# Local attention: scores for 32 queries against their 160 keys, q and k through one scratch tensor, and another order on VectorE

## The chip, the cores and the metric

The kernel runs on one core of a Trainium2 chip. The metric is the time of one execution on the device in microseconds (us). All data are float32.

## What is computed

The reference adds two blocks to x (2 sequences of 4096 tokens, 256 channels): a recurrent attention with 16 heads, and a two-layer local transformer. Only the second one is touched. Cut to it:

```
for l in range(2):                       # DEPTH
    h = shift_token(x);  q, k, v = split(h @ wqkv[l])        # 8 heads of 64
    q, k = rotary_xpos(l2norm(q) * qs, l2norm(k) * ksc)
    # windows of 128 tokens; a query sees its own window and the one before
    sim = einsum('bhwid,bhwjd->bhwij', bq * 8, bk)           # 128 x 256
    mask = (i < j) | (i > j + 128) | (j == -1)
    attn = softmax(where(mask, -max, sim));  o = attn @ bv
    x = x + o @ wo[l]
    h = layernorm(shift_token(x)) * lg + lb
    a, g = split(h @ w1[l] + b1);  x = x + (a * gelu(g)) @ w2[l] + b2
```

A query at place i sees the keys i-128 to i. So 32 neighbouring queries together see 160 keys, and 127 of the 256 places in each row of the square are masked.

## The kernel before

The program runs setup, mix, scan, gate and then local, one stage after another. The local stage (`local_stage`) works through T / 128 = 32 windows for each of two layers (NW = 32, u counts 64 of them), for two streams s = 0, 1 (the two sequences). One call of `half(s, u, w, l)` on each engine is the work on attention of stream s in window u together with the second part (values, wo, layer norm, MLP) of the other stream `o = 1 - s` in the window `um`, and the projections for the next window. There are 128 halves. `w` is the parity of the window, `un = um + 1` the other stream's next window. Each engine has its own written order of steps; semaphores tie them together.

In a half, for stream s: TensorE computes the scores of four pairs of heads (`scores`, `hp` = 0 to 3); VectorE adds the mask and takes the row maximum (`row_max`); ScalarE takes the exponent with the row sum (`exponent`); VectorE inverts the sum (`inverse_sums`), GpSimd scales P by it (`normalise`), and VectorE turns P in blocks of 32 x 32 (`turn_p`). The blocks still have to change places between groups of partitions, which goes through DRAM: SP writes two pairs at a time to scratch `pz` (`write_p`, g = 0, 1) and reads each back with four DMAs, one for 32 partitions (`read_p`). In the next half TensorE multiplies the result, `pT`, with V (`values`): pairs 0 and 1 into bank D ahead of the other stream's first scores, pairs 2 and 3 into bank B between its scores of pair 1 and pair 2.

q and k go the same way: `turn_q`, `write_q`, `read_q` and `turn_k`, `write_k`, `read_k`, through scratch `qz` and `kz`. All of these DMAs are issued by SP, in this order within a half:

```
read_q(o, un) | store, load_rot, load_window | write_p(s, u, 0)
write_k(o, un) | write_p(s, u, 1) | read_p(s, u, 0) | read_k(o, un, wn)
read_p(s, u, 1) | write_q(s, u + 1)
```

SP works in order: a DMA behind a wait is not issued before the wait is over. TensorE's order in a half is values 0 and 1 (of o), scores 0 and 1 (of s), values 2 and 3, scores 2 and 3, wo, then the projections with the mean and the variance between them (`mean` is L2529, `variance` L2533), and the MLP (L2551, L2559). `deviate` on VectorE waits for the mean.

## Time and profile before

| | |
|---|---|
| median of 3 runs | 4971.94 us (4968.18 to 4976.64) |
| the profiled execution | 4966.22 us, span 4964.4 us, mean granted TensorE clock 0.959 |
| local stage | from about 2257 us to the end |
| busy, whole span | TensorE 4507.8 us, its weight loads 3817.4, VectorE 3564.7, ScalarE 2979.7, GpSimd 2441.6 |
| DMA queue of SP | 53.1% of the 16 engines' span |

PE is TensorE, PEld its weight loads, DVE VectorE, ACT ScalarE, POOL GpSimd, SPq the DMAs that SP issues. A wait stands in brackets behind the instruction that ended it. Issuing a DMA does not count as busy time.

### The profile page before, as it was taken

The numbers are of one execution on the slowest core, as the hardware profiler recorded it, in microseconds if no ns is written. First come the engines' busy times: TensorE is split into PE (matmuls) and PEld (weight loads), VectorE is DVE, ScalarE is ACT, GpSimd is POOL, SyncE is SP. The second block draws the span as 40 slices with busy tenths as digits, with TensorE's granted clock in tenths as the row PEclk, the third lists the DMA queues.
The fourth block names the chain that finished last, engine by engine and source line by source line (L and its number), as shares of the span: only waits on it lengthen the run. The fifth ranks groups of instructions, "written<-read, shape, count | busy, mean of one in ns | idle before, by whom it ended". The sixth has DMA issues, their size and how long they took to land. (4 is left out here: it accounts for less than half of the span.)

```text
span 4964.4 us, 269505 instructions
## 1 busy us (share of the span) xinstructions
PE 4507.8 (91%) x107928; PEld 3817.4 (77%) x107928; DVE 3564.7 (72%) x10345; ACT 2979.7 (60%) x8486; POOL 2441.6 (49%) x3196
## 2 busy tenths in 40 slices
PE   7898898678888888666999999999999999999998
PEld 6888888678888888654777777777777777777777
DVE  4666666568878887475777777777777777777775
ACT  5777777534444444354666666666666666666665
POOL 1222222267777777203555555555555555555554
PEclk8999999789999999788999999999999999999999
DMA  2343343467777777694555666555565555555554
GB/s 87 87 96 93 93 98 89 114 143 165 165 165 163 167 164 161 175 299 126 170 170 168 173 174 171 172 171 171 180 196 175 173 173 172 171 171 173 173 175 131
DMA packets 1283528, 775.96 MB, mean 156 GB/s; under 512 B 686800, under 2 KB 1179088, under 8 KB 1282256
## 3 DMA queue, kind: packets, MB, share of 16 engines
q1 hardware_dynamic: 1231888, 700.43, 53.1%
q10 hardware_dynamic: 51392, 73.02, 5.0%
q14 instruction: 190, 1.56, 0.1%
q8 instruction: 58, 0.95, 0.1%
HBM read 410.44 MB, written 362.68 MB: 156 GB/s over the span
## 5 line engine op out<-in xcount | busy, mean ns | idle before, releaser
L2367 ACT ACTIVATE l_prob<-l_prob,l_nb,l_rq 128x256 f32<-128x256 f32 x1024 | 601.6, 590 | 20.8 <-DVE l_nb L2193 13.1
L2033 POOL TENSOR_TENSOR l_prob<-l_prob,l_rinv 128x512 f32<-128x512 f32 x512 | 526.8, 1039 | 108.4 <-DVE l_rinv L2173 108.4
L2017 POOL TENSOR_TENSOR l_k<-l_kn,l_tab 128x512 f32<-128x512 f32 x128 | 162.5, 1270 | 614.8 <-DVE l_kn L2165 614.8
L2559 PE MATMUL lD<-l_hid,w 128*128 128x128 f32 x3072 | 364.0, 275 | 0.0
L2559 PEld LDWEIGHTS lD<-l_hid,w 128*128 128x128 f32 x3072 | 353.3, 192 | 0.0
L2551 PEld LDWEIGHTS lA<-l_hn,w 128*128 128x128 f32 x2048 | 242.9, 195 | 110.1 <-POOL l_hn L2051 61.1
L2202 DVE STREAM_TRANSPOSE l_pb<-l_prob 128x512 f32<-128x512 f32 x512 | 326.6, 676 | 0.6 <-POOL l_prob L2033 0.5
L2027 POOL TENSOR_TENSOR l_qr<-l_q 128x512 f32<-128x512 f32 x128 | 162.4, 1269 | 328.1 <-DVE l_q L2131 328.1
L1097 POOL TENSOR_TENSOR sc_aqx<-sc_late,sc_headmask 128x256 f32<-128x256 f32 x256 | 170.8, 667 | 278.9 <-PE sc_Y L1190 277.2
L1173 PE MATMUL sc_AB<-sc_aq,sc_bkx 32*32 32x32 f32 x16384 | 257.3, 198 | 37.4 <-POOL sc_bkx L1097 29.1
L497 POOL TENSOR_TENSOR rk<-rk,bkraw 128x256 f32<-128x256 f32 x64 | 54.6, 871 | 477.9 <-DVE bkraw L383 477.9
L2551 PE MATMUL lA<-l_hn,w 128*128 128x128 f32 x2048 | 266.0, 284 | 11.8 <-POOL l_hn L2051 5.2
L1115 POOL TENSOR_TENSOR sc_bkT<-sc_tok,sc_headmask 128x128 f32<-128x128 f32 x512 | 263.2, 534 | 0.0
L2524 PE MATMUL lD<-l_oT,wo 128*128 128x128 f32 x2048 | 262.6, 281 | 0.1
L2524 PEld LDWEIGHTS lD<-l_oT,wo 128*128 128x128 f32 x2048 | 238.2, 191 | 29.2 <-issue 28.9
L2473 PE MATMUL lB<-wqkv,l_h 128*128 128x512 f32 x512 | 242.9, 597 | 17.4 <-DVE l_mask L2262 17.2
L2551 PE MATMUL lB<-l_hn,w 128*128 128x128 f32 x2048 | 250.9, 276 | 0.0
L1173 PEld LDWEIGHTS sc_AB<-sc_aq,sc_bkx 32*32 32x32 f32 x16384 | 213.3, 108 | 39.4 <-issue 38.6
L2473 PE MATMUL lC<-wqkv,l_h 128*128 128x512 f32 x512 | 241.0, 593 | 0.0
L2473 PE MATMUL lA<-wqkv,l_h 128*128 128x512 f32 x512 | 240.9, 593 | 0.0
L2551 PEld LDWEIGHTS lB<-l_hn,w 128*128 128x128 f32 x2048 | 240.5, 193 | 0.0
L2193 DVE TENSOR_TENSOR l_nb<-l_mx,l_nrq 128x2 f32<-128x2 f32 x512 | 220.6, 431 | 17.7
(276 smaller groups left out, 13707.3 us busy)
## 6 DMA issues: line engine op xcount, KB each, us to landing
scratch_pz<-l_pb SPq DMA_DIRECT2D x256, 512.0 KB, 3.0
l_pT<-scratch_pz SPq DMA_DIRECT2D x1024, 128.0 KB, 3.2
scratch_cm<-cm SPq DMA_DIRECT2D x64, 512.0 KB, 4.1
scratch_qz<-l_q SPq DMA_DIRECT2D x128, 256.0 KB, 2.9
l_qT<-scratch_qz SPq DMA_DIRECT2D x512, 64.0 KB, 2.0
scratch_kz<-l_k SPq DMA_DIRECT2D x128, 256.0 KB, 2.8
l_kT<-scratch_kz SPq DMA_DIRECT2D x512, 64.0 KB, 2.9
sc_early<-scratch_cm ACTq DMA_DIRECT2D x59, 512.0 KB, 4.7
```

The lines of the kernel that those rows point to most:

```text
L1097: return nc.gpsimd.tensor_tensor(dst[:], src.unsqueeze(2).broadcast_to([P, 2 * BG, HQ, CH]), headmask[:].unsqueeze(1).unsqueeze(3).broadca ...
L1115: last = nc.gpsimd.tensor_tensor(bkT[c % 2][:, b * BG:(b + 1) * BG], tok[k][:, c, b, 1:3].rearrange("p x g i -> p (x g) i").unsqueeze(2) . ...
L1173: last = mm(AB_ps[c][at, (x * BG + q) * QH:(x * BG + q + 1) * QH], bkx[c][at, 2 * q + x].rearrange("p h t -> p (h t)"), aq[c][at, q], star ...
L2017: tt(k1[s][:], kn[s][:], wide(2, slice(0, DH)), ALU.mult)
L2033: tt(prob[s][:, pair], prob[s][:, pair], rinv[s][:, pair].unsqueeze(2).broadcast_to([P, 2, 2 * P]), ALU.mult).then_inc(Q["pn"][s].sem, 1)
L2193: tt(nb[s][:, pair], mx[s][:, pair], nrq8[s][:, pair], ALU.mult).then_inc(Q["nb"][s].sem, 1)
L2202: nc.vector.transpose(pb[s][:, g, :, at:at + 2].rearrange("p j h x t -> p (h x) j t"), prob[s][:, 2 * hp:2 * hp + 2].rearrange("p h (x j k ...
L2367: last_ = nc.scalar.activation(prob[s][:, h], prob[s][:, h], ACT.Exp, scale=rq8[s][:, h:h + 1], bias=nb[s][:, h:h + 1], accum_out=sums[s][ ...
L2473: last_ = mm(bank[s][j][:], h[:, k * P:(k + 1) * P], wqkv[:, k, j * INNER:(j + 1) * INNER], start=(k == 0), stop=(k == CC - 1))
L2524: last_ = mm(bank[s][3][:, m * P:(m + 1) * P], wo[:, k, m * P:(m + 1) * P], oT[s][:, k], start=(k == 0), stop=(k == NHP - 1))
L2551: last_ = mm(bank[s][j][0:MW, at:at + P], w1[:, k, tile * MW:(tile + 1) * MW], hn[s][:, k], start=(k == 0), stop=(k == CC - 1))
L2559: last_ = mm(bank[s][3][:, c * P:(c + 1) * P], w2[:, m, c * P:(c + 1) * P], hid[s][:, m], start=(c == 0 and m == 0), stop=(c == CC - 1 and ...
```

## The change

- **Scores.** One matmul of 64 x 128 by 256 columns for each head becomes four of 64 x 32 by 160, one for each block i of 32 queries, into 32 partitions of the same bank. `prob`, the exponent, the scaling and the turn have 160 columns for each head instead of 256.
- **Mask.** `winmask` holds both cases, and `mask`, its preparation and `remask` are gone.
- **q and k.** Both are turned into one tile `qk`, written by one DMA to `qkz` and read by four. `qkT` holds three windows' places: the keys of a window with w = 0 are read twice, into places 2 (with q) and 0, so that the 160 keys always lie side by side.
- **P.** `pz` holds 5 blocks of 32 keys for each 32 queries. `read_p` has to place them by absolute key block in `pT`: two DMAs for each group of 32 partitions, of j + 1 and 4 - j runs.
- **VectorE's order.** `turn_k` goes ahead of `inverse_sums` 2, `turn_p` 0 ahead of `deviate`, `turn_p` 1 ahead of `inverse_sums` 3.

```diff
+    NR = BL + 1
+    SPAN = 32 * NR
...
-        qT, kT = two("qT", [P, P, NHP]), two("kT", [P, 2, BL, NHP, 32])
-        V, prob = two("V", [P, 2, HEADS, DH]), two("prob", [P, HEADS, 2 * P])
-        pb, pT = two("pb", [P, 2, BL, NHP, 2, 32]), two("pT", [P, 2, BL, NHP, 2, 32])
+        qk, qkT = two("qk", [P, BL, 2, NHP, 32]), two("qkT", [P, 3 * BL, 2, NHP, 32])
+        V, prob = two("V", [P, 2, HEADS, DH]), two("prob", [P, HEADS, SPAN])
+        pb, pT = two("pb", [P, 2, NR, NHP, 32]), two("pT", [P, 2, BL, 2, NHP, 32])
...
-                def write_q(s, u):
+                def write_qk(s, u):
 
                     sp.wait_ge(S["q_turned"][s].sem, S["q_turned"][s].after(u))
                     sp.sem_inc(sems["free"], 1)
-                    sp.wait_ge(S["qT"][s].sem, S["qT"][s].after(u, 1))
+                    sp.wait_ge(S["k_turned"][s].sem, S["k_turned"][s].after(u))
                     sp.sem_inc(sems["free"], 1)
-                    sp.dma_start(a["qz"][s], q1[s][:].rearrange("p h d -> p (h d)")).then_inc(S["q_out"][s].sem, 16)
-
-                def read_q(s, u):
-                    sp.wait_ge(S["q_out"][s].sem, S["q_out"][s].after(u))
+                    sp.wait_ge(S["qkT"][s].sem, S["qkT"][s].after(u, 1))
+                    sp.sem_inc(sems["free"], 1)
+                    if not isinstance(u, int) or u > 1:
+                        sp.wait_ge(S["kT"][s].sem, S["kT"][s].after(u - 1))
+                        sp.sem_inc(sems["free"], 1)
+                    sp.dma_start(a["qkz"][s], qk[s][:].rearrange("p j y h t -> p (j y h t)")).then_inc(S["qk_out"][s].sem, 16)
+
+                def read_qk(s, u, w):
+
+                    sp.wait_ge(S["qk_out"][s].sem, S["qk_out"][s].after(u))
                     sp.sem_inc(sems["free"], 1)
                     sp.wait_ge(Q["sc"][s].sem, Q["sc"][s].after(u * NHP - 1))
                     sp.sem_inc(sems["free"], 1)
+                    turned = a["qkz"][s].rearrange("(i c) (j n) -> j c i n", i=BL, j=BL)
+                    cur = (2, 1)[w] * BL
                     for j in range(BL):
-                        sp.dma_start(qT[s][32 * j:32 * j + 32].rearrange("p (i t) h -> p i (t h)", i=BL),
-                                     a["qz"][s].rearrange("(i c) (j n) -> j c i n", i=BL, j=BL)[j]).then_inc(S["qT"][s].sem, 16)
-
-                def write_k(s, u):
-                    sp.wait_ge(S["k_turned"][s].sem, S["k_turned"][s].after(u))
-                    sp.sem_inc(sems["free"], 1)
-                    sp.wait_ge(S["kT"][s].sem, S["kT"][s].after(u, 1))
-                    sp.sem_inc(sems["free"], 1)
-                    sp.dma_start(a["kz"][s], k1[s][:].rearrange("p h d -> p (h d)")).then_inc(S["k_out"][s].sem, 16)
-
-                def read_k(s, u, w):
-                    sp.wait_ge(S["k_out"][s].sem, S["k_out"][s].after(u))
-                    sp.sem_inc(sems["free"], 1)
-                    sp.wait_ge(Q["sc"][s].sem, Q["sc"][s].after(u * NHP - 1))
-                    sp.sem_inc(sems["free"], 1)
-                    for j in range(BL):
-                        sp.dma_start(kT[s][32 * j:32 * j + 32, w].rearrange("p i h t -> p i (h t)"),
-                                     a["kz"][s].rearrange("(i c) (j n) -> j c i n", i=BL, j=BL)[j]).then_inc(S["kT"][s].sem, 16)
+                        sp.dma_start(qkT[s][32 * j:32 * j + 32, cur:cur + BL].rearrange("p i y h t -> p i (y h t)"),
+                                     turned[j]).then_inc(S["qkT"][s].sem, 16)
+                    if w == 0:
+                        for j in range(BL):
+                            sp.dma_start(qkT[s][32 * j:32 * j + 32, 0:BL, 1].rearrange("p i h t -> p i (h t)"),
+                                         turned[j][:, :, 32 * NHP:]).then_inc(S["kT"][s].sem, 16)
...
+                    n, row = 32 * NHP, 32 * NHP * NR
+                    at = (s * 2 + g) * P * row
                     for j in range(BL):
-                        sp.dma_start(pT[s][32 * j:32 * j + 32, g].rearrange("p i h x t -> p i (h x t)"),
-                                     a["pz"][s, g].rearrange("(i c) (j n) -> j c i n", i=BL, j=BL)[j]).then_inc(H[g]["pT"][s].sem, 16)
+                        for slot, lo, hi in ((0, 0, j + 1), (1, j, BL)):
+                            start = at + lo * 32 * row + (j + BL * slot - lo) * n
+                            sp.dma_start(pT[s][32 * j:32 * j + 32, g, lo:hi, slot].rearrange("p i h t -> p i (h t)"),
+                                         bass.AP(a["pz"].tensor, start, [[row, 32], [32 * row - n, hi - lo], [1, n]])
+                                         ).then_inc(H[g]["pT"][s].sem, 16)
...
-                    if within(un):
-                        read_q(o, un)
...
                     write_p(s, u, 0)
                     if within(un):
-                        write_k(o, un)
+                        write_qk(o, un)
                     write_p(s, u, 1)
                     read_p(s, u, 0)
                     if within(un):
-                        read_k(o, un, wn)
+                        read_qk(o, un, wn)
                     read_p(s, u, 1)
...
-                    if within(u + 1):
-                        write_q(s, u + 1)
...
-                        for t in (kT[s], V[s]):
+                        for t in (qkT[s], V[s], pT[s]):
                             nc.gpsimd.memset(t[:], 0.0)
                         nc.gpsimd.memset(hid[s][:, FULL, :], 0.0)
                         nc.gpsimd.memset(x1[s][1][:], 0.0)
-                        nc.gpsimd.memset(mask[s][0][:], MASKED)
...
+                    dve.wait_ge(S["qk_out"][s].sem, S["qk_out"][s].after(u, 1))
+                    nc.vector.transpose(qk[s][:, :, 0].rearrange("p j h t -> p h j t"),
...
-                                                               in1=mask[s][w][:].rearrange("p x n -> p (x n)"), scale=1.0, scalar=3 * MASKED,
+                                                               in1=wm[:, int(u in (0, NW))], scale=1.0, scalar=3 * MASKED,
...
-                    nc.vector.transpose(pb[s][:, g, :, at:at + 2].rearrange("p j h x t -> p (h x) j t"),
-                                        prob[s][:, 2 * hp:2 * hp + 2].rearrange("p h (x j k) -> p (h x) j k", x=2, j=BL)
+                    nc.vector.transpose(pb[s][:, g, :, at:at + 2].rearrange("p r h t -> p h r t"),
+                                        prob[s][:, 2 * hp:2 * hp + 2].rearrange("p h (r k) -> p h r k", r=NR)
...
-                def remask(s, u, w):
-                    if w == 0:
-                        at = u if isinstance(u, int) else None
-                        dve.wait_ge(Q["mx"][s].sem, Q["mx"][s].after(u * NHP + NHP - 1))
-                        if at == NW - 2:
-                            nc.vector.memset(mask[s][0][:, 1, :], MASKED).then_inc(S["mask0"][s].sem, 2)
-                        else:
-                            nc.vector.tensor_copy(mask[s][0][:, 1, :], wm[:, 0:P]).then_inc(S["mask0"][s].sem, 2)
...
                     inverse_sums(s, u, 1)
+                    if within(un):
+                        turn_k(o, un)
                     inverse_sums(s, u, 2)
+                    turn_p(s, u, 0)
                     if mlp:
                         deviate(o, um, wm_)
+                    turn_p(s, u, 1)
                     inverse_sums(s, u, 3)
-                    turn_p(s, u, 0)
-                    turn_p(s, u, 1)
-                    if within(un):
-                        turn_k(o, un)
                     turn_p(s, u, 2)
                     turn_p(s, u, 3)
...
-                    for x in range(2):
-                        rows_ = slice(x * DH, (x + 1) * DH)
-                        last_ = mm(scored(s, hp, x), qT[s][rows_, :, hp], kT[s][rows_, :, :, hp].rearrange("p x i t -> p (x i) t"),
-                                   start=True, stop=True)
+                        pe.sem_inc(sems["free_pe"], 1)
+                    own, back = (2, 1)[w] * BL, (1, 0)[w] * BL
+                    for i in range(BL):
+                        for x in range(2):
+                            rows_ = slice(x * DH, (x + 1) * DH)
+                            last_ = mm(scored(s, hp, x)[32 * i:32 * i + 32], qkT[s][rows_, own + i, 0, hp],
+                                       qkT[s][rows_, back + i:back + i + NR, 1, hp], start=True, stop=True)
                     last_.then_inc(Q["sc"][s].sem, 1)
...
-                            last_ = mm(valued(s, hp)[x * DH:(x + 1) * DH], V[s][:, slot, 2 * hp + x], pT[s][:, g, :, at + x, slot],
+                            last_ = mm(valued(s, hp)[x * DH:(x + 1) * DH], V[s][:, (1 - w, w)[slot], 2 * hp + x], pT[s][:, g, :, slot, at + x],
...
-    q, kx = np.arange(P)[:, None], np.arange(P)[None, :]
-    neg = np.float32(MASKED)
-    before, own = np.where(kx < q, neg, 0), np.where(kx > q, neg, 0)
-    out["winmask"] = np.concatenate([before, own], axis=1).astype(np.float32)
+    row, r = np.arange(P)[:, None], np.arange(160)[None, :]
+    neg, behind = np.float32(MASKED), r - row % 32
+    near = np.where((behind < 0) | (behind > P), neg, 0)
+    begin = np.where(r < P - row // 32 * 32, neg, near)
+    out["winmask"] = np.stack([near, begin], axis=1).astype(np.float32)
```

SP's DMAs of one half in the local stage, before. The names are out<-in; behind them stands the shape, in which 32x4x256 is 32 partitions by 4 runs of 256 elements:

```order
L1924 DMA scratch_pz<-l_pb 128x1024
L1907 DMA scratch_kz<-l_k 128x512
L1924 DMA scratch_pz<-l_pb 128x1024
L1932 DMA l_pT<-scratch_pz 32x4x256 x4
L1915 DMA l_kT<-scratch_kz 32x4x128 x4
L1932 DMA l_pT<-scratch_pz 32x4x256 x4
L1891 DMA scratch_qz<-l_q 128x512
```

The same place with the change, in a half with wn = 0 (in the others L1912 is missing), up to the start of the second read of P, which has the same seven rows as the first:

```order
L1921 DMA scratch_pz<-l_pb 128x640
L1897 DMA scratch_qkz<-l_qk 128x1024
L1921 DMA scratch_pz<-l_pb 128x640
L1933 DMA l_pT<-scratch_pz 32x128
L1933 DMA l_pT<-scratch_pz 32x4x128
L1933 DMA l_pT<-scratch_pz 32x2x128
L1933 DMA l_pT<-scratch_pz 32x3x128 x2
L1933 DMA l_pT<-scratch_pz 32x2x128
L1933 DMA l_pT<-scratch_pz 32x4x128
L1933 DMA l_pT<-scratch_pz 32x128
L1908 DMA l_qkT<-scratch_qkz 32x4x256 x4
L1912 DMA l_qkT<-scratch_qkz 32x4x128 x4
```

Between the writes of P and the second read of P stood 8 reads; now 12 or 16 stand there, and the second read is 8 itself.

VectorE between the residual sum of the other stream (`attended`) and the end of the turns of P, before:

```order
L2219 TENSOR_TENSOR l_x_0<-lD,l_h_0 128x2x128
L2173 RECIPROCAL l_rinv<-l_sums 128x2 x2
L2228 TENSOR_TENSOR l_dev<-l_x_0,lD 128x256
L2173 RECIPROCAL l_rinv<-l_sums 128x2
L2202 STREAM_TRANSPOSE l_pb<-l_prob 128x4x4x32 x2
L2158 STREAM_TRANSPOSE l_k<-l_kr 128x4x4x32
L2202 STREAM_TRANSPOSE l_pb<-l_prob 128x4x4x32 x2
```

The same with the change:

```order
L2202 TENSOR_TENSOR l_x_0<-lD,l_h_0 128x2x128
L2167 RECIPROCAL l_rinv<-l_sums 128x2
L2152 STREAM_TRANSPOSE l_qk<-l_kr 128x4x4x32
L2167 RECIPROCAL l_rinv<-l_sums 128x2
L2194 STREAM_TRANSPOSE l_pb<-l_prob 128x2x5x32
L2211 TENSOR_TENSOR l_dev<-l_x_0,lD 128x256
L2194 STREAM_TRANSPOSE l_pb<-l_prob 128x2x5x32
L2167 RECIPROCAL l_rinv<-l_sums 128x2
L2194 STREAM_TRANSPOSE l_pb<-l_prob 128x2x5x32 x2
```

The turn of k and of pair 0 now stand ahead of the deviation (`l_dev`), that of pair 1 right behind it.

## Rows read from the trace of the kernel before

**Rows 1.** The head of the page
```profile
span 4964.4 us, 269505 instructions
```

**Rows 2.** Windows, 3000 to 3600 us: busy us PE, PEld, DVE, ACT, POOL; clock
```profile
3000.00:3600.00 600.00, 593.89 (x4349) 464.02 (x4350) 441.36 (x1503) 396.95 (x1083) 325.98 (x366) 1.00 0.59 173
```

**Rows 3.** PE timeline, one half and the next: start us, us, what, [idle before <-releaser]
```profile
3515.77 1.09 PE L2516 MATMUL lD<-l_pT,l_V 128*64 128x128 f32 x16
3516.80 0.60 PE L2498 MATMUL lB<-l_kT,l_qT 64*128 64x256 f32 x1
...
3517.47 0.63 PE L2498 MATMUL lA<-l_kT,l_qT 64*128 64x256 f32 x4
3518.72 1.09 PE L2516 MATMUL lB<-l_pT,l_V 128*64 128x128 f32 x16 [0.62 <-DMA l_pT<-scratch_pz]
...
3520.99 2.05 PE L2524 MATMUL lD<-l_oT,wo 128*128 128x128 f32 x16
...
3524.60 0.38 PE L2529 MATMUL lD<-l_x1s,l_mean_w 128*128 128x128 f32 x2
...
3539.83 1.09 PE L2516 MATMUL lB<-l_pT,l_V 128*64 128x128 f32 x16 [1.06 <-DMA l_pT<-scratch_pz]
```

**Rows 4.** Timeline of DVE in the same half
```profile
3525.02 0.42 DVE L2228 TENSOR_TENSOR l_dev<-l_x,lD 128x256 f32<-128x256 f32 x1 [1.07 <-PE lD L2529]
...
3525.43 1.28 DVE L2202 STREAM_TRANSPOSE l_pb<-l_prob 128x512 f32<-128x512 f32 x2
```

**Rows 5.** Timeline of SP's queue in the same half
```profile
3526.87 0.34 SPq L1924 DMA_DIRECT2D scratch_pz<-l_pb  x1
...
3531.39 1.74 SPq L1932 DMA_DIRECT2D l_pT<-scratch_pz  x4
3533.32 1.73 SPq L1915 DMA_DIRECT2D l_kT<-scratch_kz  x4
3535.22 1.73 SPq L1932 DMA_DIRECT2D l_pT<-scratch_pz  x4
```

**Rows 6.** First and last start of the value matmuls (source view of their line)
```profile
L2516 PE MATMUL lD<-l_pT,l_V x2048: 272/273/476, 2308.1 to 4940.7; 128*64 128x128 f32 x187
```

**Rows 7.** Waits of PE, 2400 to 4900 us: total, times, longest
```profile
PE lB L2516 <- DMA l_pT<-scratch_pz: 6.8, 11, 1.3
```

**Rows 8.** One read of P on SP (source view): ns min/median/max
```profile
L1932 SPq DMA_DIRECT2D l_pT<-scratch_pz x1024: 302/432/1631, 2303.0 to 4935.4; - x171
```

**Rows 9.** DMA issues of the page: KB each, median us to landing
```profile
scratch_pz<-l_pb SPq DMA_DIRECT2D x256, 512.0 KB, 3.0
l_pT<-scratch_pz SPq DMA_DIRECT2D x1024, 128.0 KB, 3.2
...
l_qT<-scratch_qz SPq DMA_DIRECT2D x512, 64.0 KB, 2.0
```

**Rows 10.** The page's costliest groups: busy us, mean ns of one
```profile
L2367 ACT ACTIVATE l_prob<-l_prob,l_nb,l_rq 128x256 f32<-128x256 f32 x1024 | 601.6, 590 | 20.8 <-DVE l_nb L2193 13.1
L2033 POOL TENSOR_TENSOR l_prob<-l_prob,l_rinv 128x512 f32<-128x512 f32 x512 | 526.8, 1039 | 108.4 <-DVE l_rinv L2173 108.4
...
L2202 DVE STREAM_TRANSPOSE l_pb<-l_prob 128x512 f32<-128x512 f32 x512 | 326.6, 676 | 0.6 <-POOL l_prob L2033 0.5
...
L1173 PE MATMUL sc_AB<-sc_aq,sc_bkx 32*32 32x32 f32 x16384 | 257.3, 198 | 37.4 <-POOL sc_bkx L1097 29.1
```

**Rows 11.** Timeline of SP in the scan stage: four DMAs of 512 runs each
```profile
1518.32 2.35 SPq L1025 DMA_DIRECT2D sc_part<-scratch_inv  x4
```

**Rows 12.** PE timeline in the gate stage, before the local stage
```profile
2225.66 1.89 PE L1707 MATMUL ga_O<-ga_wos,ga_z 128*128 128x256 f32 x8
...
2230.44 1.11 PE L1699 MATMUL ga_Y<-ident,ga_yt 128*128 128x128 f32 x4 [2.36 <-DMA ga_yt<-scratch_y_tok]
2231.34 3.09 PE L1707 MATMUL ga_O<-ga_wos,ga_z 128*128 128x256 f32 x8
```

**Rows 13.** GpSimd's timeline at the start of the local stage
```profile
2256.95 0.95 POOL L2069 MEMSET l_kT<- 128x1024 f32 x1 [225.59 <-POOLq L104]
```

More of the change, by code:

```diff
@@ L1761, in local_stage @@
         rot, tab = two("rot", [P, 4, DH]), two("tab", [P, 4, DH])
-        wm = one("wm", [P, 2 * P])
+        wm = one("wm", [P, 2, SPAN])
         mean_w, pause, least = one("mean_w", [P, P]), one("pause", [P, NB]), one("least", [P, 1])
         x1s, dsqs = two("x1s", [P, P]), two("dsqs", [P, P])
-        mask = [two(f"mask{s}_", [P, 2, P]) for s in range(NB)]
         hT = [two(f"h{s}_", [P, CC, P + 1]) for s in range(NB)]
@@ L1780, in local_stage @@
         bank = [[ctx.enter_context(nc.psum_tensor(f"l{n}{s}", [P, 512], F32)) for n in "ABCD"] for s in range(NB)]
-        sems = {n: ctx.enter_context(nc.semaphore(f"l_{n}")) for n in ("wm", "set", "prep", "zero", "free", "wqkv", "wo", "w1", "w2", "wiped0", "wiped1")}
+        sems = {n: ctx.enter_context(nc.semaphore(f"l_{n}")) for n in ("wm", "set", "zero", "free", "free_pe", "wqkv", "wo", "w1", "w2", "wiped0", "wiped1")}
         R = signals(nc, ctx, "tab", 1, "lr")
         S = signals(nc, ctx, "q_ps k_ps v_ps qsq ksq v_sb ss_q ss_k clamped ln_n rn rq8 kn qm qr k12 kr q_turned k_turned "
-                    "q_out:16 k_out:16 qT:64 kT:64 mask0 wo_ps carry x1 x1_sum mean_ps dev dsq dsq_sum var_ps ln_v rstd hn w2_ps hout "
+                    "qk_out:16 qkT:64 kT:32 wo_ps carry x1 x1_sum mean_ps dev dsq dsq_sum var_ps ln_v rstd hn w2_ps hout "
                     "out:16", 2, "l")
@@ L1789, in local_stage @@
         O = signals(nc, ctx, "oT", 2, "lg", ahead=4)
-        H = [signals(nc, ctx, "p_out:16 pT:64", 2, f"lg{g}_") for g in range(2)]
+        H = [signals(nc, ctx, "p_out:16 pT:128", 2, f"lg{g}_") for g in range(2)]
         I = [signals(nc, ctx, "h_in:8 rot_in:8", 2, f"li{w}_") for w in range(2)]
@@ L1846, in scored @@
         def scored(s, hp, x):
-            return ((bank[s][1], bank[s][2]), (bank[s][0], bank[1 - s][0]))[hp % 2][x][:, 0:2 * P]
+            return ((bank[s][1], bank[s][2]), (bank[s][0], bank[1 - s][0]))[hp % 2][x][:, 0:SPAN]
         def valued(s, hp):
@@ L2015, in rotate_k @@
                     pool.wait_ge(S["kr"][s].sem, S["kr"][s].after(u, 1))
-                    pool.wait_ge(S["k_out"][s].sem, S["k_out"][s].after(u, 1))
                     tt(k1[s][:], kn[s][:], wide(2, slice(0, DH)), ALU.mult)
@@ L2032, in normalise @@
                     pair = slice(2 * hp, 2 * hp + 2)
-                    tt(prob[s][:, pair], prob[s][:, pair], rinv[s][:, pair].unsqueeze(2).broadcast_to([P, 2, 2 * P]), ALU.mult
+                    tt(prob[s][:, pair], prob[s][:, pair], rinv[s][:, pair].unsqueeze(2).broadcast_to([P, 2, SPAN]), ALU.mult
                        ).then_inc(Q["pn"][s].sem, 1)
@@ L2125, in rotate_q @@
                     dve.wait_ge(S["qr"][s].sem, S["qr"][s].after(u, 1))
-                    dve.wait_ge(S["q_out"][s].sem, S["q_out"][s].after(u, 1))
                     q = bank[s][0][:].rearrange("p (h d) -> p h d", h=HEADS)
@@ L2157, in turn_k @@
                     dve.wait_ge(S["kr"][s].sem, S["kr"][s].after(u))
-                    nc.vector.transpose(k1[s][:].rearrange("p h d -> p (h d)").rearrange("p (j h t) -> p h j t", j=BL, h=NHP),
+                    dve.wait_ge(S["qk_out"][s].sem, S["qk_out"][s].after(u, 1))
+                    nc.vector.transpose(qk[s][:, :, 1].rearrange("p j h t -> p h j t"),
                                         kr[s][:].rearrange("p h d -> p (h d)").rearrange("p (h j c) -> p h j c", h=NHP, j=BL)
@@ L2181, in row_max @@
                     dve.wait_ge(Q["p_turned"][s].sem, Q["p_turned"][s].after(n, NHP))
-                    if hp == 0 and w == 0:
-                        dve.wait_ge(S["mask0"][s].sem, S["mask0"][s].after(u, 1))
                     nc.vector.memset(pause[:, s:s + 1], 0.0)
@@ L2260, in first @@
                     for s in range(NB):
-                        nc.vector.tensor_copy(mask[s][0][:, 0, :], wm[:, P:2 * P])
-                        last = nc.vector.tensor_copy(mask[s][1][:].rearrange("p x n -> p (x n)"), wm[:])
-                    last.then_inc(sems["prep"], 1)
-                    dve.wait_ge(sems["prep"], 1)
-                    for s in range(NB):
                         sum_k(s, 0)
@@ L2480, in scores @@
                     if hp == 0:
-                        pe.wait_ge(S["qT"][s].sem, S["qT"][s].after(u))
-                        pe.wait_ge(S["kT"][s].sem, S["kT"][s].after(u))
+                        pe.wait_ge(S["qkT"][s].sem, S["qkT"][s].after(u))
+                        pe.sem_inc(sems["free_pe"], 1)
+                        if w == 1:
+                            pe.wait_ge(S["kT"][s].sem, S["kT"][s].after(u))
+                            pe.sem_inc(sems["free_pe"], 1)
                         pe.wait_ge(M["hid"][s].sem, M["hid"][s].after(3 * (u - 1) + 2))
+                        pe.sem_inc(sems["free_pe"], 1)
                         if at(s, u, s, NW):
@@ L2624, in last @@
                     for hp in range(NHP):
-                        values(s, u, hp, 1)
+                        values(s, u, w, hp, 1)
                     turn_out(1 - s, u)
```

31 lines of the change are left out of this document (15 added, 16 removed).

## Prediction

> **What bounds the kernel now.** The change touches the local stage only, so I read the execution from there. Windows over a quiet stretch come first: TensorE is busy 593.89 of 600 us at granted clock 1.00, the other engines at most 464 [rows 2]. The stage is made of 128 halves; value matmuls start from 2308.1 to 4940.7, which spans 127 of them, so (4940.7 - 2308.1) / 127 = 20.7 us a half [rows 6]. That looks like a kernel that only TensorE's work can shorten. Next the timeline of TensorE over one half [rows 3]. It is not free of waits: the second batch of value matmuls (bank B, heads 4 to 7 of the other stream) waits 0.62 us for the read of P in one half and 1.06 in the next. The table of waits has 11 such waits, 6.8 us in all, the longest 1.3 [rows 7]. So a second loop runs a hair under TensorE's. I call the start of that batch V. In this half V is 3518.72, the next V is 3539.83: the loop took 21.11 us, and TensorE would have been ready at 3538.77, after 20.05 us.
>
> The loop, followed through the engines: V, the scores of pairs 2 and 3, wo at 3520.99, the mean at 3524.60 [rows 3]; the deviation on VectorE at 3525.02, then the turns of pairs 0 and 1 [rows 4]; SP writes them at 3526.87, which is V + 8.15, waits until the write has landed, and from 3531.39 issues three bursts of four reads, P's first half, k, P's second half, until 3536.95 [rows 5]; the last read lands 3.2 us after its issue began [rows 9], and V can start. SP's issuing is 5.56 us of this loop. The page does not count it as busy time of any engine, so no share of busy time shows it.
>
> **The change part by part.**
> *Arithmetic off TensorE.* 160 of 256 columns are left in the exponent, the row maximum, the scaling by 1/sum and the turns of P. At durations in proportion a scaling goes from 1039 ns to about 650 to 750, a turn from 676 to about 430 [rows 10]. ScalarE, GpSimd and VectorE have slack in rows 2, so this is worth nothing of itself; it counts only as far as it moves the write of P in the loop.
> *Scores on TensorE.* Pairs 0 and 1 take 1.30 us now (3516.80 to 3518.10), pairs 2 and 3 about the same [rows 3]. Each pair becomes 8 tiles of 64 rows by 32 columns over 160 columns. No row shows such a tile. Bound from below: all 8 at once, in proportion 160/256 of the streaming. For the rate of issue the nearest row is the 32*32 tiles of the scan, 16384 matmul records in 257.3 us, 16 ns each [rows 10]: 32 records for two pairs are 0.5 us, less than now. I take 1.0 us for two pairs, 0.6 us less in a half. Bound from above: the four query blocks one after another, which is a rival below. TensorE's own period becomes 19.45 here; over all halves, 0.6 under the mean of 20.7 with its few waits taken off, about 19.7.
> *VectorE's order.* The deviation waits for the mean, V + 6.3 now. With the scores of pairs 2 and 3 0.3 us shorter it starts at V + 6.0 and ends at V + 6.4. Pair 0 is turned ahead of it, only pair 1 behind it: V + 6.85, and SP writes at V + 7.0. That is 1.15 us earlier than in this half. The turn of k goes into the idle time of 1.07 us before the deviation [rows 4], at no cost; if that idle time were gone it would cost its 0.7 us.
> *q and k in one trip.* One write and one burst of four for both. The burst of q stood outside the loop, that of k inside; the new one takes k's place, 1.73 us as before [rows 5]. In every window with an even number four more reads lay the keys down a second time: 1.9 us more, and they stand ahead of the second half of P. Such a half I call long, the others short.
> *The reads of P.* Here the sum turns. Each half of P is now read by 8 DMAs instead of 4, each of 1 to 4 runs for 32 partitions, for 20 runs instead of 32. What does an issue cost? 302 ns for the first of a burst, 432 for the others (median), and some 40 between: 1.74 for four [rows 5, 8]. Does a smaller DMA issue faster? Four DMAs of 512 runs each take 2.35 us, or 0.59 each [rows 11], against 0.43 for 128 runs: four times the runs, a third more time, 0.4 ns a run. Down to 80 runs on average that gives 0.02 less. So eight take 3.5 us. Bound from below: all at the 302 + 40 of the first, 2.7 us. The landing should shorten: reads of 512-byte runs land in 2.0 us against 3.2 [rows 9], because the traffic behind each is smaller.
>
> The sum for the loop, short half: 7.0 to the write; 2.8 for its landing (3.0 in the page [rows 9], and its rows are 2,560 bytes instead of 4,096); 3.5 + 0.2 + 1.73 + 0.2 + 3.5 issuing; 1.6 from the end of the last issue to its landing (2.0 less 0.43). That is 20.5. Long half: 22.4. Mean 21.45 against 20.7 now, both above TensorE's 19.7: TensorE would stand idle 0.8 us ahead of V in a short half and 2.7 in a long one.
> *The clock.* In the gate stage one idle time of 2.36 us was followed by matmuls at half speed, eight of them in 3.09 us instead of 1.89 [rows 12]: the granted clock had gone from 2.4 to 1.2 GHz. An idle time of 2.7 us in a long half may do the same, and what follows V is in the loop: up to 3.4 us of work at half clock, 1.7 us longer. I count it for one long half in four, 0.2 us a half on average.
> Sum: (21.45 + 0.2 - 20.7) x 127 = +121 us. At the stage's start GpSimd clears 3,840 more elements per partition in each of two streams, at 0.95 us for 1024 [rows 13] 7 us; the mask's preparation goes, which stood behind it, and I count +5 together. On the profiled execution's own time, 4966.2 us (span 4964.4 [rows 1]), this gives 5092; the median of the runs shown is 5.7 above that execution. I round to **5090 us**.
>
> The Trainium skill, "DMA: Bandwidth & Descriptors", section "Issuing engines are not separate DMA queues", says that the time to initiate a DMA is usually small relative to the DMA itself. By that the eight extra reads would be free. Here 1.73 us of issuing for four stands against a landing of 2.0, and in a chain of three bursts it is the larger part; the same page does say that many descriptors can be emitted before their cost shows, which agrees with 0.43 against 0.59.
>
> **The rivals.**
> *Small DMAs issue fast, faster than before (0.27).* Eight reads take 2.7 us each burst. Short: 7.0 + 2.8 + 2.7 + 0.2 + 1.73 + 0.2 + 2.7 + 1.6 = 18.9, under TensorE's 19.7, which then sets it; long 20.8. Mean 20.25, -0.45 x 127 = -57, 4912 us; with all loops under TensorE, -127, 4845. For it: nothing in the rows has fewer than 128 runs. Against it: 0.43 and 0.59 lie on a nearly flat line. It decides from about 0.37 us an issue down, where the mean loop falls to 20.7.
> *The same mechanism with the clock down in most long halves, or the tiles of the scores one block after another (0.12).* The clock in every long half: +0.65 more a half, +82, about 5170. Blocks in turn: 4 x 2 x 160 columns a pair, about 1.15 us against 0.6, for four pairs +2.2 us a half, of which 1.1 is inside the loop; mean loop about 22.9, 5270 us. For it: the value matmuls' two column tiles do run together, but no row has four column tiles on 64 rows. The Trainium skill, "TensorEngine Tiling (Array Packing)", section "Key Properties", says that tiles operate independently; by that page the blocks run together.
> *No difference (0.06).* The issue at about 0.37 us.
>
> **How the numbers follow.** My forecast has 0.55. Its own range is 5020 (no clock loss, write 0.4 us earlier) to 5180. The range for 8 in 10 goes down into the fast rival, whose likeliest value is 4912, and up to the clock in every long half: 4905 to 5190. Within 0.2% is 10 us, about what a measurement of this kernel can tell from no change. Slower: 0.55 + 0.12 = 0.67; same 0.06; faster 0.27.
>
> **What would show it.** The page of the changed kernel should have TensorE waiting for the read of P ahead of the second value batch in nearly every half, 0.5 to 1 us and 2 to 3 us in turn; SP's bursts of eight at 3.5 us; the write at V + 7; the last read landing 2.0 us after its issue; the scores of two pairs in 1.0 us; VectorE, ScalarE and GpSimd with smaller shares. I am wrong if a burst of eight takes under 3 us, if the waits of TensorE are for something else (the scores for q and k, whose read should land 7 us behind the landing of P's write, V + 16.8, in time for the scores), or if the scores take longer than 1.3.

## The result, and the profile after

The changed kernel takes **5171.1 us** (median of 4 runs, 5165.24 to 5176.03) against 4970.4 for the kernel before (4 runs beside it, 4968.18 to 4976.64): ratio 1.0401, 95% interval 1.0383 to 1.0419. It is slower by 201 us, where 121 were forecast.

The quiet stretch of the local stage in both traces. First the windows view of the changed kernel, 3000 to 3600 us (columns as in [rows 2]):
```profile
3000.00:3600.00 600.00, 534.64 (x5282) 408.22 (x5281) 350.95 (x1375) 347.38 (x999) 266.97 (x337) 0.96 0.42 127
```
TensorE is busy 534.64 of 600 us where it was busy 593.89, its granted clock is 0.96 instead of 1.00, and VectorE, ScalarE and GpSimd have all lost share, as they should with less to do. Next what TensorE waits for, 2400 to 5100 us (total, times, longest):
```profile
PE lB L2504 <- DMA l_pT<-scratch_pz: 232.0, 121, 4.4
PE lB L2486 <- issue: 17.2, 44, 0.8
PE lB L2486 <- DMA l_qkT<-scratch_qkz: 11.7, 12, 1.6
```
The wait for P's rows that had 6.8 us in 11 places [rows 7] has 232.0 us in 121: in nearly every half. A timeline of TensorE over one short and one long half shows it at work (the scores' matmuls are cut to the last row of each batch):
```profile
3508.55 0.29 PE L2486 MATMUL lB<-l_qkT 64*32 64x160 f32 x1 [1.06 <-DMA l_qkT<-scratch_qkz]
...
3510.47 1.09 PE L2504 MATMUL lB<-l_pT,l_V 128*64 128x128 f32 x16 [1.09 <-DMA l_pT<-scratch_pz]
3511.49 0.32 PE L2486 MATMUL lB<-l_qkT 64*32 64x160 f32 x1
...
3511.79 0.48 PE L2486 MATMUL lA<-l_qkT 64*32 64x160 f32 x16
3512.20 2.05 PE L2512 MATMUL lD<-l_oT,wo 128*128 128x128 f32 x16
...
3533.70 1.98 PE L2504 MATMUL lB<-l_pT,l_V 128*64 128x128 f32 x16 [4.27 <-DMA l_pT<-scratch_pz]
...
3536.14 0.78 PE L2486 MATMUL lA<-l_qkT 64*32 64x160 f32 x16
3536.86 3.38 PE L2512 MATMUL lD<-l_oT,wo 128*128 128x128 f32 x16
```
At 3510.47 the second batch has waited 1.09 us and runs at full clock: 1.09 us for 16 matmuls, wo in 2.05. At 3533.70 it has waited 4.27 us, and what follows runs at 1.2 GHz (granted clock 0.50 from 3533.7 to 3539): 1.98 and 3.38 us for the same rows. SP's queue over the same time says why the wait is so long:
```profile
3517.24 0.34 SPq L1921 DMA_DIRECT2D scratch_pz<-l_pb  x1
...
3519.59 3.79 SPq L1933 DMA_DIRECT2D l_pT<-scratch_pz  x8
3523.56 1.73 SPq L1908 DMA_DIRECT2D l_qkT<-scratch_qkz  x4
3525.33 1.85 SPq L1912 DMA_DIRECT2D l_qkT<-scratch_qkz  x4
3527.36 4.98 SPq L1933 DMA_DIRECT2D l_pT<-scratch_pz  x8
...
3543.22 0.34 SPq L1921 DMA_DIRECT2D scratch_pz<-l_pb  x1
```
The write starts 6.77 us behind V = 3510.47, and SP then issues without a pause from 3519.59 to 3532.34: 24 DMAs, 12.75 us, where [rows 5] had 12 in 5.56. The next write stands 9.52 us behind V = 3533.70: that is the half at the low clock. The wait of 4.27 us and the 9.52 are larger than usual, since these halves lie in a straight piece of program between the stage's two loops (more on it under filler_wide): the last burst took 4.98 us where its median is 3.62, and the idle time before V is 2.98 us in the mean behind a long half. The rows that answer to [rows 10] and [rows 9], from the page (groups; issues with us to landing):
```profile
L2344 ACT ACTIVATE l_prob<-l_prob,l_nb,l_rq 128x160 f32<-128x160 f32 x1024 | 518.3, 509 | 14.4 <-DVE l_nb L2185 14.4
L2027 POOL TENSOR_TENSOR l_prob<-l_prob,l_rinv 128x320 f32<-128x320 f32 x512 | 363.3, 720 | 268.8 <-DVE l_rinv L2167 268.6
```
```profile
scratch_pz<-l_pb SPq DMA_DIRECT2D x256, 320.0 KB, 2.5
...
l_pT<-scratch_pz SPq DMA_DIRECT2D x512, 64.0 KB, 2.0
```

The loop of the prediction, term by term. Each value is a mean over the halves of the profiled execution, taken from the starts and ends of the rows named: V (second value batch), the write of P's first half, its first and last read, the first and last read of the second half.

| us a half | before | forecast | after |
|---|---|---|---|
| V to the write of P | 8.49 | 7.0, +0.2 for the clock | 7.61 |
| write to the first read | 2.92 | 2.8 | 2.42 |
| first burst of P | 1.87 | 3.5 | 3.90 |
| between the bursts (q and k) | 2.16 | 3.1 | 3.17 |
| second burst | 1.76 | 3.5 | 3.73 |
| end of issuing to the next V | 3.49 | 1.6 | 1.47 |
| period | 20.70 | 21.65 | 22.28 |

(22.28 - 20.70) x 127 = 201 us. The two profiled executions differ by 209.7 us in their spans, and the other 9 lie ahead of the first V, which starts at 2321.0 instead of 2312.1 (the first value batch of all at 2311.7 instead of 2308.1 [rows 6], 3.6 us, where 5 were forecast for the start). Nothing outside the local stage is needed.

### The profile page after: what moved, and what is told of

It reads as the page before. It is cut to its first block and busy times, and to the rows that moved or that the text cites. A ratio compares the mean times of both kernels' runs of the same rounds, so it can differ in the third digit from the quotient of the medians.

```text
span 5174.1 us, 282935 instructions
## 1 busy us (share of the span) xinstructions
PE 4445.7 (86%) x114072; PEld 3735.2 (72%) x114072; DVE 3282.7 (63%) x10277; ACT 2890.7 (56%) x8486; POOL 2287.0 (44%) x3196
## 5 line engine op out<-in xcount | busy, mean ns | idle before, releaser
L2344 ACT ACTIVATE l_prob<-l_prob,l_nb,l_rq 128x160 f32<-128x160 f32 x1024 | 518.3, 509 | 14.4 <-DVE l_nb L2185 14.4
L2027 POOL TENSOR_TENSOR l_prob<-l_prob,l_rinv 128x320 f32<-128x320 f32 x512 | 363.3, 720 | 268.8 <-DVE l_rinv L2167 268.6
L2504 PE MATMUL lB<-l_pT,l_V 128*64 128x128 f32 x2048 | 164.6, 311 | 242.5 <-DMA l_pT<-scratch_pz 242.5
L2353 ACT COPY l_oT<-lB 128x256 f32<-128x256 f32 x128 | 47.7, 373 | 519.1 <-PE lB L2504 519.1
L2504 PEld LDWEIGHTS lB<-l_pT,l_V 128*64 128x64 f32 x2048 | 127.5, 153 | 278.3 <-DMA l_pT<-scratch_pz 278.2
L2194 DVE STREAM_TRANSPOSE l_pb<-l_prob 128x320 f32<-128x320 f32 x512 | 250.7, 498 | 104.3 <-POOL l_prob L2027 104.3
L2512 PEld LDWEIGHTS lD<-l_oT,wo 128*128 128x128 f32 x2048 | 283.0, 222 | 46.3 <-issue 27.0
L2178 DVE CUSTOM_DVE_ANT_0 l_prob<-lB,l_wm 128x160 f32<-128x160 f32 x256 | 81.8, 320 | 361.8 <-issue 341.0
L2512 PE MATMUL lD<-l_oT,wo 128*128 128x128 f32 x2048 | 307.4, 311 | 0.1
```

The source lines that it names most:

```text
L2027: tt(prob[s][:, pair], prob[s][:, pair], rinv[s][:, pair].unsqueeze(2).broadcast_to([P, 2, SPAN]), ALU.mult).then_inc(Q["pn"][s].sem, 1)
L2194: nc.vector.transpose(pb[s][:, g, :, at:at + 2].rearrange("p r h t -> p h r t"), prob[s][:, 2 * hp:2 * hp + 2].rearrange("p h (r k) -> p h ...
L2344: last_ = nc.scalar.activation(prob[s][:, h], prob[s][:, h], ACT.Exp, scale=rq8[s][:, h:h + 1], bias=nb[s][:, h:h + 1], accum_out=sums[s][ ...
L2504: last_ = mm(valued(s, hp)[x * DH:(x + 1) * DH], V[s][:, (1 - w, w)[slot], 2 * hp + x], pT[s][:, g, :, slot, at + x], start=(slot == 0), s ...
L2512: last_ = mm(bank[s][3][:, m * P:(m + 1) * P], wo[:, k, m * P:(m + 1) * P], oT[s][:, k], start=(k == 0), stop=(k == NHP - 1))
```

## The experiments

Nine kernels ran, each beside the kernel before, whose median was 4967.9, 4966.0 and 4964.5 us in the three groups. All are named by what they change.

**before_8reads: the kernel before, with each read of P split in two.** Nothing else of the change is in it.
```diff
-  sp.dma_start(pT[s][32 * j:32 * j + 32, g]..., a["pz"][s, g]...[j])
+  for i in range(0, BL, 2):
+      sp.dma_start(pT[s][32 * j:32 * j + 32, g, i:i + 2]..., a["pz"][s, g]...[j][:, i:i + 2])
```


> The kernel before, with each of the four reads of a half of P split into two of two runs each: same bytes, same runs, eight more DMAs issued by SP in a half, nothing else. Theory (the issue on SP is the length that counts): a burst of eight takes 3.6 us instead of 1.74, the loop from one second value batch to the next grows by 3.7 us less the 0.4 of slack it had, so +3.3 x 127 = +420 us, 5390, and up to 100 more from TensorE's clock. Rival (small transfers are hidden; the time went elsewhere in the change): within 20 us of 4970.

Measured 5295.0 us, ratio 1.0646 (1.0624 to 1.0667). Twice the issues for the same bytes cost 327 us: more than the whole change, and 95 less than the 5390 expected. The bursts went from 1.87 and 1.76 to 3.78 and 3.66 us, V to the write from 8.49 to 9.14 (the clock), the period to 23.28. What the expectation left out is the tail from the last issue to V, which fell from 3.50 to 1.65 us; 1.2 of these 1.85 us are that reads of half the size land after 2.0 us instead of 3.2. The windows view, 3000 to 3600, has the clock at 0.95:
```profile
3000.00:3600.00 600.00, 544.77 (x3845) 424.04 (x3844) 389.73 (x1335) 351.20 (x957) 288.77 (x324) 0.95 0.47 151
```

**keys_last: the changed kernel, with the keys laid down the second time behind P's last reads** instead of ahead of them. The same DMAs, in another order on SP.
```diff
 read_p(s, u, 1)
+if within(un):
+    read_back(o, wn)     # the "if w == 0" loop, taken out of read_qk
```


> The changed kernel, with the second laying down of the keys (four reads in every window with w = 0) behind the second half of P instead of ahead of it. Theory: long halves lose 1.9 us of their loop, half of the halves, -120 us, and the waits of TensorE fall to about 1 us, so that its clock stays up and the 0.6 us a half that the write of P came late go too, -75 us: 4980 to 5050. Rival (the clock or the eight reads alone hold the loop): -50 us at most.

Measured 4970.4 us, ratio 1.0005 (0.9994 to 1.0015): the whole loss is gone, and the time is 10 us under the range. Between the bursts 2.22 us instead of 3.17, V to the write 6.91 instead of 7.61. Of the 206 us between the two profiled spans (5174.1 and 4968.2), 0.95 x 127 = 121 are the issuing itself and 0.70 x 127 = 89 the clock, which falls in the longer wait. In the view of waits (2400 to 5100) and the windows:
```profile
PE lB L2510 <- DMA l_pT<-scratch_pz: 114.9, 121, 3.3
```
```profile
3000.00:3600.00 600.00, 555.51 (x5684) 424.97 (x5684) 378.46 (x1484) 374.47 (x1073) 287.46 (x363) 0.99 0.45 139
```
The batch waits as often as in the changed kernel but half as long, and the clock stays up.

**old_order: the changed kernel with VectorE's old order** (k and the first two pairs turned behind the deviation).
```diff
-turn_k(o, un); inverse_sums(s, u, 2); turn_p(s, u, 0); deviate(...); turn_p(s, u, 1); inverse_sums(s, u, 3)
+inverse_sums(s, u, 2); deviate(...); inverse_sums(s, u, 3); turn_p(s, u, 0); turn_p(s, u, 1); ...; turn_k(o, un)
```


> The changed kernel with VectorE's order of before: both turns and the turn of k behind the deviation and the last inverse. Theory (the write of P is in the loop): it comes 0.5 to 0.6 us later, +65 to +75 us, 5240. Rival (the order does nothing, as the bursts of reads are what counts): within 10 us of 5171.

Measured 5252.2 us, ratio 1.0573 (1.0555 to 1.0590): the new order is worth 81 us. V to the write 8.24 against 7.61, the rest alike.

**keys_last_old_order: both of these edits together.** It has the DMAs of before_8reads ahead of V, one for one, and its order on VectorE; between the two lie the 160 columns instead of 256, the smaller writes and rows, and one round trip for q and k.

> The changed kernel with the second laying down of keys behind the last reads of P and with VectorE's old order: the same eight reads of P, two writes and four other reads ahead of the second batch as before_8reads had, and the same order on VectorE. What is left between the two is the arithmetic on 160 keys instead of 256, the smaller write of P, and one round trip for q and k instead of two. My theory: this part of the change is worth a lot by itself. In the loop of the keys_last kernel the write of P comes at V+6.85; the old order puts it 0.6 us later, the half goes from 20.6 to 21.3 us, and with a little more clock loss the time is 5040 to 5090 us, 200 to 260 below before_8reads (5295). Rival: narrower scores and tiles lie under other work and are worth nothing: 5200 or more.

Measured 5022.7 us, ratio 1.0107 (1.0090 to 1.0124), 18 us under the range. V to the write 7.49 against 9.14, write to read 2.44 against 2.92, period 21.10 against 23.28. So this part is worth 272 us once the loop over P is the bound, though none of it lay on a busy engine's path before. The kernels in a chain, by their medians: 4970.4 (before), +325 for twice as many reads, -272 for the narrow scores and P, -52 for VectorE's order, +201 for the second laying down of the keys ahead of P's second half, 5171.1. The medians of the kernel before in the groups that this chain crosses differ by up to 6 us, so each link is good to about that.

**filler: the changed kernel, with matmuls that compute nothing put ahead of the second value batch**, to keep TensorE busy in its wait: 14 small ones in long halves, 4 in short ones, in the bank that the batch overwrites. The wait that frees this bank moves ahead of them.
```diff
+if hp == 2:
+    for _ in range(fill):     # fill: 14 or 4
+        mm(bank[s][1][:, 0:P], mean_w[:], mean_w[:], start=True, stop=True)
```


> The changed kernel with matmuls added whose result is written over: 14 of 128x128x128 (about 3 us) where TensorE waits for P in halves with a long wait, 4 (0.9 us) in the others, into the part of bank B that the value matmuls then overwrite. Theory (the clock falls in these waits and makes the path to the write of P longer): the granted clock in the stage is 1.00 and the write comes at V + 6.8 in all halves, not in half of them, -0.6 to -0.8 us a half, 5070 to 5095. Rival (the clock costs nothing beyond the wait): 5171, or more by what the added work takes.

Measured 5243.7 us, ratio 1.0547 (1.0519 to 1.0576): a miss, 73 us slower than without the filler. V to the write did fall to 6.86, in all halves but one. But the bursts rose to 4.18 both and the tail to 1.94. I formed the theory that the added instructions were at fault, and tried the same with few.

**filler_wide: four matmuls of 512 columns in long halves, one in short ones.**
```diff
+    for _ in range(fill):     # fill: 4 or 1
+        mm(bank[s][1][:], mean_w[:], rows[:, 0:512], start=True, stop=True)
```


> The changed kernel with wide matmuls of 512 columns put ahead of the second batch of value matmuls, into the bank that this batch overwrites: four of them in the halves whose wait is long and one in the others, so the program grows by few instructions. They compute nothing that is used. My theory: the short filler's loss came from its many instructions and not from keeping TensorE busy. So V to the write of P stays near 6.8 us in all halves (7.6 in the mean before), the granted clock in the loop is 1.00, the two bursts of P's reads stay at 3.9 and 3.7 us, and the loop loses 0.6 to 0.8 us a half: 5020 to 5070 us against 5171. First rival: keeping TensorE busy doesn't pay, as in the short filler, because work in the wait delays the batch when the data lands earlier than the fill ends: 5150 to 5240. Second rival: the clock falls nonetheless: about 5170.

Measured 5229.3 us, ratio 1.0528 (1.0511 to 1.0546): a miss again, and only 14 us better with far fewer added instructions, so their number is not what counts. The trace takes the miss apart. The stage has two loops with a straight piece between them. Windows of filler_wide over the first loop, the straight piece and the second loop:
```profile
2470.00:3400.00 930.00, 921.66 (x8666) 667.02 (x8666) 561.37 (x2196) 557.16 (x1595) 425.83 (x537) 1.00 0.43 131
3500.00:3900.00 400.00, 381.50 (x3564) 275.64 (x3562) 236.18 (x904) 226.43 (x646) 181.10 (x228) 1.00 0.45 141
4030.00:4950.00 920.00, 846.83 (x7732) 609.12 (x7731) 524.06 (x1989) 494.20 (x1420) 405.16 (x519) 0.96 0.40 124
```
and of the changed kernel over the same:
```profile
2470.00:3400.00 930.00, 834.96 (x8292) 638.61 (x8291) 548.76 (x2150) 545.85 (x1563) 416.56 (x526) 0.97 0.42 129
3500.00:3900.00 400.00, 345.04 (x3326) 263.49 (x3326) 224.28 (x869) 216.40 (x624) 171.24 (x216) 0.93 0.43 131
4030.00:4950.00 920.00, 847.32 (x8381) 644.49 (x8378) 580.14 (x2198) 545.32 (x1565) 446.11 (x569) 0.97 0.44 135
```
In the first loop the filler does what was expected: the period falls from 21.98 to 21.55 us, V to the write from 7.51 to 6.81, the bursts stay at 3.84 and 3.64. Of the 0.70 us that the write gains 0.26 is lost in the tail to V, 1.66 instead of 1.40. In the second the period rises from 21.84 to 24.18, the bursts to 4.42 and 4.19. What differs is a queue that moves instructions. The DMA view of filler_wide, 4030 to 4950, has it:
```profile
q8 instruction: 85, 1.39, 0.7%
```
In the first loop this queue moves nothing; in the changed kernel neither loop shows it, only the straight piece (27 packets). In the short filler it is the other way round, 89 packets and a period of 23.63 in the first loop, 25 and 22.01 in the second. TensorE's waits in filler_wide's second loop (4030 to 4950) have a row that only the two fillers have; in the short one's first loop it has 34.0 us in 10 places:
```profile
PE lD L2507 <- issue: 49.5, 18, 3.8
```
It stops up to 3.8 us for nothing that the profile shows. So the loops in which this queue moves packets all the time are 1.7 and 2.3 us a half slower than the same loops of the changed kernel, on TensorE and in SP's bursts, and the filler buys 0.4. That the packets are the cause is not shown: no run changes them alone. Nor can I tell from these traces why one loop has them and the other not.

**qk_on_act: keys_last, with the four reads of q and k issued by ScalarE** between its squares and the first gelu.
```diff
-read_qk(o, un, wn)                 # on SP, between read_p(s, u, 0) and read_p(s, u, 1)
+read_qk(o, un, wn)                 # on ScalarE, ahead of gelu(o, um, 0, ...)
```


> The changed kernel with the second laying down of keys behind the last reads of P (as in keys_last) and the four reads of q and k issued by ScalarE between its squares and its first gelu, instead of by SyncE between the two bursts of P's reads. My theory: what bounds the changed kernel is the chain of issues on SyncE between the landing of P's write and the second batch. Taking 2.2 us out of it (20.64 a half in keys_last) makes 18.5, less than what TensorE needs by itself, so the half comes to 19.3 to 19.8 us and the kernel to 4700 to 4800 us; the wait of the second batch for P's rows falls below 1 us. First rival: the issues delay ScalarE's gelus by 1.7 us and with them the gates and the second MLP product, which gives half or all of it back: 4850 to 4970. Second rival: small transfers share the queues' capacity whoever issues them, so the bursts only stretch: about 4970 (as keys_last).

Measured **4908.6 us**, ratio 0.9883 (0.9867 to 0.9900): faster than both kernels, 62 us under keys_last, but 109 above the range. SP's two bursts stand 0.22 us apart, and the wait of the second batch for P is gone from the view of waits (one of 0.3 us is left). In its place, 2400 to 5100:
```profile
PE lD L2556 <- DVE l_hid L2215: 51.5, 99, 2.2
```
TensorE waits for the last gate. ScalarE's timeline shows what comes ahead of it:
```profile
3418.80 0.60 ACT L2309 ACTIVATE l_sqq<-lA 128x512 f32<-128x512 f32 x1 [1.01 <-PE lA L2459]
3419.63 2.82 ACTq L2328 DMA_DIRECT2D l_qkT<-scratch_qkz  x4
3422.54 1.28 ACT L2388 ACT_TABLE_LOAD   x1 [3.13 <-issue]
```
The four issues stand between the square and the gelu. They take 1.76 us in the median; the 2.82 shown is among the longest. The first rival had this mechanism. The period is 20.21 us, to which P adds nothing and the clock (0.99 from 3000 to 3600) next to nothing.

**qk_on_act_old_order: the same with VectorE's old order.**

> As qk_on_act, but with VectorE's old order (the keys and the first two pairs of P turned behind the deviation). My theory: where TensorE bounds the half, the order on VectorE no longer sets the end, so it is within 20 us of qk_on_act (it cost 81 us in the changed kernel, whose end hangs on P's write). Rival: the chain over P still sets the end, and the old order costs 60 to 90 us here too.

Measured 4972.7 us, ratio 1.0015 (1.0006 to 1.0025): 64 us slower than qk_on_act, so my theory fell. TensorE's wait for the last gate grew to 110.8 us. The traces say why: k is turned later, so the write of q and k lands at V + 11.07 instead of V + 10.60 (medians), and ScalarE, whose square ends at V + 10.32 in both kernels, starts its reads at V + 11.09 instead of V + 10.62, with the gelus behind them. That is 0.47 us later, and the period is 0.50 longer. No run tests it by itself.

**qk_on_act_split: qk_on_act, with two of the four reads behind the last gelu.**

> As qk_on_act, but ScalarE issues only two of the four reads of q and k ahead of the first gelu and the other two behind the last one. My theory: in qk_on_act TensorE's wait for the last gate (51.5 us over the middle of the program, 99 times) comes from ScalarE's 1.7 us of issues ahead of the gelus; halving them ends nearly all of that wait, and the scores' wait for q and k stays small, since the last reads land about 0.5 us ahead of them: 0.3 to 0.5 us a half, 4840 to 4880 us against 4909. Rival: the last two reads land late and the scores wait for them instead: 4900 to 4950.

Measured 4911.8 us, ratio 0.9895 (0.9879 to 0.9912): the same as qk_on_act, and the rival was right. Most of the wait for the gate went, and the scores' wait for q and k came (2400 to 5100):
```profile
PE lB L2498 <- DMA l_qkT<-scratch_qkz: 46.4, 55, 1.5
PE lB L2498 <- issue: 28.3, 54, 0.8
PE lD L2559 <- DVE l_hid L2215: 13.5, 11, 2.7
```

## Why the prediction was right, and where it was off

**The bound.** Right. The loop V, P's write, the reads on SP, V ran a hair under TensorE's own period before, and it is what the change lengthened. before_8reads shows it alone: DMAs of half the size, no byte and no instruction of another engine more, 327 us.

The forecast's own range, 5020 to 5180, holds the result near its upper end. The wide range, 4905 to 5190, would have held a faster kernel too, so it proves little; the mechanism rests on the loop's terms below and on the runs.

**The reads of P.** Right in kind. The price of an issue hardly falls with the size of the DMA: median 429 ns for a read of P now, 432 before [rows 8]. The sum 3.5 was too low by 0.4 and 0.2. It priced the second four with a cheap first issue as well, but only the first of the eight is cheap (median 317 ns): 0.36 us to the second start, six steps of 0.471 and 0.43 for the last make 3.6, which is the median of the second burst, 3.62. The first burst is 3.82 in the median, because its second and third issues take 559 and 462 ns there; in the kernel before, too, the first burst was the longer one (1.82 against 1.73), and the prediction went by one half in which both took 1.74 and 1.73. Why the first is longer, no run shows. The last 0.1 of both means comes from outside the loops, most of it from the straight piece, where the bursts take 4.17 and 4.05. There the whole period is 23.95 us against 21.9 in the loops; over its 19 halves this is 0.3 of the 0.6 us by which the forecast of the period was short, but part of that is the clock (0.93 there) and is counted again below. The fast rival needed 0.37 us an issue and is refuted.

**The Trainium skill,** "DMA: Bandwidth & Descriptors", section "Issuing engines are not separate DMA queues", calls the time to initiate a DMA usually small relative to the DMA. For one DMA that holds here, 0.43 us against a landing of 2.0. But the issues of one queue add up and their landings overlap: sixteen issues of P took 7.6 us of the loop, and V started 1.47 us after the last issue ended. The same section says that another issuing engine saves just that time; there the trace agrees: 2.0 us less between the bursts in qk_on_act. The prediction also took from this page that many descriptors can be emitted before their cost shows; the page says that of the path of DMAs issued by GpSimd, and those here are SP's, so 0.43 against 0.59 stands on the rows alone.

**The landing of the reads,** 1.8 to 2.0 us instead of 3.2, was right, but 512-byte runs are not the reason. The page before has the reads of k, of the same size as those of q, at 2.9 us; in before_8reads P's reads have runs of 1,024 bytes and land in 2.0, and the reads of k, unchanged, stand between them and land in 2.0 as well. So the size of the DMAs around a read counts.

**The keys' second reads** at 1.9 us in a long half: right (1.85 in the row of L1912; 0.95 in the mean of both, by keys_last). Idle time of TensorE ahead of V was to be 0.8 us in short and 2.7 in long halves, and is 0.82 and 2.98.

**The clock: this is the term that was mis-sized most.** The prediction had it fall in one long half in four, 0.2 us a half. The mechanism and its price when it happens were right: the write comes at V + 6.8 at full clock and typically at V + 8.4 when it has fallen, 1.6 us against the 1.7 forecast, for which the prediction named no row (of [rows 12], eight matmuls give 3.09 - 1.89 = 1.2 us). Its frequency was not: after idle times of over 2 us ahead of V, 58 of 66 writes came later than V + 7.9, after shorter ones 1 of 60. So it happens in nearly every long half, and costs 0.8 us a half (7.61 against 6.8). Of the 80 us that the forecast fell short, (0.8 - 0.2) x 127 = 76 would be this alone. The two bursts fell short by as much, 0.6 us a half, and other terms gave that back (below). The clock in most long halves is what the second rival said, at 5170; that its number was met within 1 us is luck, since it had the bursts, the landing and the write as the forecast had them. Its other half, the scores' query blocks in turn, is refuted: the eight 64*32 tiles of a pair, two heads by four blocks, all start between 3511.49 and 3511.54.

**The terms that offset each other.** The write at V + 6.8 instead of 7.0 (scores of two pairs in 0.78 us, 3511.49 to 3512.27, where 1.0 was taken), the landing of P's write 0.4 shorter and the tail 0.1, against the bursts' 0.6. TensorE's own period, 19.7 in the prediction, does not follow from its working: 20.7 less 0.6 for the scores and less 6.8 us of waits spread over 120 halves is 20.0. The value is right all the same, by luck: the scores save 1.04 us a half, and the period of qk_on_act, 20.21, less its 67 us of waits over 123 halves, is 19.7.

**VectorE's order and the arithmetic** were costed as moving only P's write. That holds in the main: of the 2.18 us between before_8reads and keys_last_old_order the write is 1.65, and the shorter landing of its smaller rows 0.48. At full clock they moved the write from 8.49 in the mean to 6.8, 0.54 more than the 1.15 forecast; 0.34 of that is only that the prediction started from one half with 8.15. At the new bound each tenth of it counts: 81 us for the order, 272 for the narrow scores and P together. Behind the measured +201 stand a gain of 324 us (272 + 52) and a loss of 526 (325 + 201).

## What to carry to other kernels

- Count the issues that one queue makes between a write and the last read that someone waits for, and multiply them by the time of one issue, not by bytes. A cut in bytes that doubles the DMAs can cost more than it saves; what nobody waits for belongs behind what somebody does.
- Where the idle time of TensorE grows from under 1 us to 3, price the low clock in all such places, and look whether what follows the wait is itself in the loop.
- A gain on engines that are not the bound is not lost: look whether it shortens the loop that will be the bound next.

## What the runs showed of the hardware

- Issues on SP: 0.43 us each for reads of 1 to 4 runs a partition as for those of 4, the first of a burst 0.32 in both kernels. The second of the first burst took 0.56 in the changed kernel, for no reason that a run shows.
- The landing of a read depends on its neighbours in the queue: the reads of k, 64 KB each, took 2.9 us between reads of 128 KB (before) and 2.0 between reads of 64 KB (before_8reads).
- Filling a wait with idle matmuls keeps the granted clock at 1.00 (filler_wide, first loop), but both kernels with it were slower. The loops in which the instruction queue q8 moves packets all through (85 and 89 of them) were slower by 2.3 us a half in filler_wide (second loop) and by 1.7 in the short filler (first loop); that the packets cause it is not shown.
- The tail from the last issue to V is 1.47 us with all reads on SP's queue and 2.86 with those of q and k on ScalarE's at the same time: in the page the reads of P land after 2.4 to 2.6 us instead of 1.8 to 2.0. So the reads of P landed about 0.6 us later with reads of 128 KB under way on the other queue. It costs nothing there: the second batch no longer waits for P, and the rest of the 2.86 is TensorE coming later than the rows.
